# Row sums of |w_fc| taken by VectorE instead of ScalarE in a two-layer gated transformer kernel

## What is computed

```python
def _bitlinear(x, w_latent):
    scale = clip(mean(abs(w_latent), axis=1, keepdims=True), 1e-05, None)
    tern = clip(round(w_latent / scale), -1.0, 1.0)
    w = w_latent + stop_gradient(tern - w_latent)
    return x @ (w * scale).T

h = _bitlinear(x, w_fc) + gate * (x @ v.T @ fast_b.T @ u.T)
r = maximum(h, 0.0)
return _bitlinear(r * r, w_proj)
```

## Time and profile before

| | us |
|---|---|
| median of three runs | 1175.09 |
| lowest and highest | 1174.94, 1177.23 |
| span of the profiled execution, first to last instruction | 1176.7 |
| PE busy in it | 1094.3 (93%) |
| DVE busy | 953.5 (81%) |
| ACT busy | 799.4 (68%) |

### The profile page before, as it was taken

One profiled execution on the slowest core, in us unless ns is written; L12 is line 12 of the kernel. 1 busy time (PEld: TensorE's weight loads), 2 busy tenths in 40 slices (PEclk: granted clock), 3 DMA queues, 4 the chain that ended last, 5 costly groups with the idle time before them and its releaser, 6 DMA issues.

```text
span 1176.7 us, 22172 instructions
## 1 busy us (share of the span) xinstructions
PE 1094.3 (93%) x8270; PEld 677.4 (58%) x8558; DVE 953.5 (81%) x1989; ACT 799.4 (68%) x1575; POOL 591.5 (50%) x567
## 2 busy tenths in 40 slices
PE   5776699999999999999899999999999999999997
PEld 5544456474655656475655656475656656564654
DVE  4796868778789888788878798898879886998667
ACT  3988947676683958576584857676674957586545
POOL 4243545464653746454544656555545555564431
PEclk9888799999999999999999999999999999999999
DMA  9959651434525343533625252443436242432210
GB/s 339 367 153 309 204 122 47 99 81 77 126 59 117 69 116 73 104 81 68 126 53 136 57 123 68 89 110 77 108 55 145 45 119 61 103 69 55 68 45 27
DMA packets 273802, 128.11 MB, mean 109 GB/s; under 512 B 247568, under 2 KB 248080, under 8 KB 272016
## 3 DMA queue, kind: packets, MB, share of 16 engines
q1 hardware_dynamic: 273136, 125.73, 41.8%
q10 hardware_dynamic: 560, 0.96, 0.3%
HBM read 57.19 MB, written 8.39 MB: 56 GB/s over the span
## 4 chain that ended last, share of the span: by engine, by line
PE 55%; ACT 17%; DVE 16%; POOL 5%; issue 4%; DMA 2%; SPq 0%; ACTq 0%; DVEq 0%
PE ps L1861 14%; PE ps L1835 10%; PE ps L1904 6%; PE ps L1920 5%; PE ps L1788 5%; ACT e L966 4%; PE ps L1735 4%; PE ps L1883 4%; ACT rl L1002 3%; ACT hid L1007 2%; ACT sq L1013 2%; PE ps L1760 1%; DVE st L1369 1%; PE ps L1841 1%; PE ps L1775 1%
## 5 line engine op out<-in xcount | busy, mean ns | idle before, releaser
L1835 PE MATMUL ps<-xT,fcT 128*128 128x256 f16 x2048 | 262.5, 276 | 10.8 <-ACT rl L1002 7.1
L749 POOL TENSOR_TENSOR rs<-ve,nhalf 128x1 f32<-128x1 f32 x160 | 101.7, 638 | 306.1 <-DVE ve L1374 222.8
L1861 PE MATMUL ps<-pjT,hid 128*128 128x512 fp8e4 x1024 | 232.3, 379 | 2.6 <-POOL hid L776 1.6
L1835 PEld LDWEIGHTS ps<-xT,fcT 128*128 128x128 fp8e4 x2048 | 200.1, 99 | 52.6 <-ACT rl L1002 10.0
L776 POOL TENSOR_TENSOR hid<-sq,hid 128x512 f16<-128x512 f32 x128 | 163.1, 1279 | 80.3 <-ACT sq L1013 79.4
L1861 PEld LDWEIGHTS ps<-pjT,hid 128*128 128x128 f16 x1024 | 98.0, 98 | 98.3
L1002 ACT ACTIVATE rl<-ps,rsf 128x256 f32<-128x256 f32 x256 | 106.4, 469 | 25.0 <-PE ps L1841 24.8
L966 ACT ACTIVATE e<-ps,nmb,sig 128x128 f32<-128x128 f32 x256 | 113.1, 462 | 7.2 <-DVE nmb L1412 6.9
L1904 PE MATMUL ps<-w1T,q4T 128*128 128x512 fp8e4 x480 | 114.2, 379 | 0.7 <-issue 0.6
L1058 ACT ACTIVATE q<-h 128x2048 f16<-128x2048 f32 x30 | 57.3, 1910 | 79.3 <-DVE h L1531 79.3
L781 POOL TENSOR_TENSOR e<-e,einv 128x512 f32<-128x512 f32 x64 | 70.1, 1100 | 78.5 <-DVE einv L1416 78.5
(11 more groups left out here) (243 smaller groups left out, 2025.7 us busy)
## 6 DMA issues: line engine op xcount, KB each, us to landing
xb<-in_x SPq DMA_DIRECT2D x16, 512.0 KB, 3.6
xa<-in_x SPq DMA_DIRECT2D x15, 512.0 KB, 4.0
out<-r SPq DMA_DIRECT2D x30, 256.0 KB, 2.3
rope<-in_rope SPq DMA_DIRECT2D x16, 384.0 KB, 3.2
h<-in_w1T SPq DMA_DIRECT2D x6, 1024.0 KB, 5.8
h<-in_w2T SPq DMA_DIRECT2D x6, 1024.0 KB, 6.4
h<-in_wkvT SPq DMA_DIRECT2D x2, 1024.0 KB, 12.6
hid<-in_w_fc SPq DMA_DIRECT2D x2, 1024.0 KB, 9.9
```

The costliest lines, as they stand in the source:

```text
L1835: pe.matmul(ps[:, FFN0 + m % 2, a * G:(a + 1) * G], fcT[:, k, f * P:(f + 1) * P], xT2[:, xs, k, :], start=(xs == 0 and k == 0), stop=False)
L1861: mm = pe.matmul(ps[:, FFN0 + t, :], hid[:, xs, c, t * P:(t + 1) * P], pjT[:, c, :], start=(c == 0 and xs == 0), stop=(c == FC - 1 and xs ...
```

## The change

`row_sums` and its four places on ACT are gone, with the semaphore `c_rows`. `row_scales` on DVE now makes the sums of a "fc" piece itself, with one reduction over a view of 4 x 512 elements per partition, in front of scale and reciprocal, as it did for "pj". It waits for the piece's transfer instead of for ACT. The place numbers of all other steps are as they were, and no transfer is moved. The order of PE, POOL and SP is the same, instruction by instruction.

```diff
@@ PREP, ACT @@
-                     evac=(6, 14, 15, 29, 33, 35, 36, 37), rows=(4, 7, 10, 21), whole=(5, 8, 12, 28), low=(32,),
+                     evac=(6, 14, 15, 29, 33, 35, 36, 37), whole=(5, 8, 12, 28), low=(32,),
@@ ACT @@
-            def row_sums(q):
-
-                i = QUANT[q][1]
-                arrived(act, q)
-                src = piece[PLACE[q]]
-                for c in range(KC):
-                    done = KC * i + c
-                    if done > 0:
-                        act.wait_ge(c_rows, done)
-                    act.activation(lowA[:, c * D:(c + 1) * D], src[:, c * D:(c + 1) * D], ACT.Abs,
-                                   accum_out=scf[:, done:done + 1]).then_inc(c_rows, 1)
...
-                for q in here("ACT", "rows", p):
-                    row_sums(q)
                 for _ in here("ACT", "low", p):
-                    act.wait_ge(c_rows, FC)
@@ DVE, row_scales @@
                 kind, i = QUANT[q]
+                arrived(dve, q)
+                src = piece[PLACE[q]]
                 if kind == "fc":
                     sc, cols = scf[:, 4 * i:4 * i + 4], slice(4 * i, 4 * i + 4)
-                    dve.wait_ge(c_rows, KC * (i + 1))
+                    src = src.rearrange("p (c n) -> p c n", c=KC)
                 else:
                     sc, cols = scd[:, i:i + 1], slice(FC + i, FC + i + 1)
-                    arrived(dve, q)
-                    dve.tensor_reduce(sc, piece[PLACE[q]], axis=AX.X, op=ALU.add, apply_absolute_value=True).then_inc(c_rowd, 1)
-                    dve.wait_ge(c_rowd, i + 1)
+                dve.tensor_reduce(sc, src, axis=AX.X, op=ALU.add, apply_absolute_value=True).then_inc(c_rowd, 1)
+                dve.wait_ge(c_rowd, q + 1)
```

More of the change, by code:

```diff
@@ L258, in build @@
          c_krot, c_wmax, c_mxd, c_mxps, c_mx, c_wscale, c_whi, c_wlo, c_vrep, c_kvmax, c_kvinv, c_kap, c_khi, c_klo,
-         c_vhi, c_vlo, c_cs, c_csb, c_cps, c_cb, c_tanh, c_wchain, c_scale, c_b2, c_rows, c_thr, c_rowd, c_quant, c_quantg,
+         c_vhi, c_vlo, c_cs, c_csb, c_cps, c_cb, c_tanh, c_wchain, c_scale, c_b2, c_thr, c_rowd, c_quant, c_quantg,
          c_tern, c_quantp, c_lowps, c_low, c_lowzero, c_lowF, c_lowt, c_lowact, c_bnd, c_rsf, c_scd,
@@ L263, in build @@
             "c_wmax c_mxd c_mxps c_mx c_wscale c_whi c_wlo c_vrep c_kvmax c_kvinv c_kap c_khi c_klo "
-            "c_vhi c_vlo c_cs c_csb c_cps c_cb c_tanh c_wchain c_scale c_b2 c_rows c_thr c_rowd c_quant c_quantg c_tern c_quantp "
+            "c_vhi c_vlo c_cs c_csb c_cps c_cb c_tanh c_wchain c_scale c_b2 c_thr c_rowd c_quant c_quantg c_tern c_quantp "
             "c_lowps c_low c_lowzero c_lowF c_lowt c_lowact c_bnd c_rsf c_scd c_scps c_sc c_asum "
```

## The result

| | before | after |
|---|---|---|
| median of five runs, us | 1177.23 | 1184.04 |
| lowest and highest, us | 1174.94, 1179.34 | 1182.16, 1185.53 |
| span of the profiled execution, us | 1176.7 | 1181.9 |

The changed kernel is slower by a ratio of 1.0057, 95% interval 1.0040 to 1.0074: +6.7 us, between 4.7 and 8.7. The prediction said 1180.0 with a range of 1176.9 to 1181.6. The direction was right and the mechanism mostly too. The size was too small, and the range did not hold the time. The five runs of before include the three of the table ahead of the prediction, whose median was 1175.09, 2.1 us lower.

A forecast was written before the change was run, and what follows sets the result against it. PE, busy 93% of the span, was read as the bound, the change acting in the first 92 us. Terms +2.7, first collision +0.4, second +1.8 made +4.9 on 1175.1: 1180.0 us, range 1176.9 to 1181.6.

The forecast's parts named there:

- the 0.4 kept for it: VectorE's four-result reduction was taken as 2.3 us a piece; 0.4 us more per piece was kept for the range.
- here lies the trap: Piece 2: sums stand behind the maximum of v, which waits for PE; 1.4 us late at the scores of group 0.
- piece 3: No VectorE gap: 2.3 us in full, 3.7 us late; PE's mix covers 1.0, leaving 2.7 at the first w_proj sum.
- The first collision: First subtraction of P on VectorE starts 0.16 us before GpSimd's normalisation, which takes 0.4 us more.
- second collision: Third subtraction of P on VectorE held by GpSimd's w_proj conversion; VectorE stands still 2 us, +1.8 in the sum; chance 0.47.
- The race: At 77.4, GpSimd's conversion starts ahead of VectorE's third subtraction of P by 0.1 us or less.
- The "faster" rival: ScalarE's relief reaches the path at pieces 1 and 2, -0.7 us each; 1172 to 1173.7 us; chance 0.08.
- PE starts its transposes ... 0.5 us late: Piece 0: k's second rotation is pushed back about 0.5 us, so the first ternary block starts 0.5 us late.
- PE is now 0.5 late, so 37.9: Piece 2: the maximum of v, started when PE finishes v, moves from 37.38 to 37.9.
- the clock only behind 92 us: At 92.5 to 94 us PE's granted clock is 0.54; other waits could move that slow stretch a microsecond either way.
- The extra hold at the products behind v: Rival: GpSimd's second x16a subtraction holds two VectorE tensor_scalars behind the maximum of v; +0.95 us, 1180.9; no separate chance.
- If the delay at 91 us is not found at the end: Sign of being wrong: the delay at the last block of transposes, about 91 us, should reach the run's end one to one.

The follow-up runs named there:

- f4: Against e3, its eight extra PE matmuls included: GpSimd's second x16a subtraction moved behind its first sum of q's rotation; 1183.0 us, ratio 1.0058 to the kernel before.
- f1: Kernel before with piece 3's sums alone on VectorE, at the place of the change; 1179.27 us, +0.31%.
- e2: Changed kernel with piece 2's sums on VectorE moved ahead of the maximum of v; 1182.63 us, ratio 1.0049 to the kernel before.
- e3: Changed kernel with eight unused matmuls on PE behind the projection of k, before the first ternary block; 1184.89 us, ratio 1.0071 to the kernel before.
- f2: Changed kernel with piece 0's sums on VectorE moved ahead of the low half of wq; 1183.35 us, ratio 1.0064 to the kernel before.
- h1: Kernel before with piece 1 alone on VectorE, ScalarE's piece 2 passes moved up, GpSimd's second x16a subtraction moved later; 1176.53 us, ratio 0.9996.
- e4: Changed kernel with the third subtraction of P moved behind the sums of the second w_proj piece; 1180.87 us, +0.37% on the kernel before.
- f3: Changed kernel with piece 3's sums moved up into VectorE's gap after the second rotation of q; 1179.12 us, +0.19% on the kernel before.
- g1: Kernel before with the sums of pieces 1 and 2 shared, two blocks each on ScalarE and VectorE; 1177.29 us, +0.10%, interval around zero.
- g2: Changed kernel with eight extra PE matmuls, GpSimd's second x16a subtraction later, piece 3's sums in the gap after q's second rotation; 1179.95 us, +0.33% on the kernel before.
- g3: Kernel before with piece 3's sums alone on VectorE, in the gap after the second rotation of q; 1179.26 us, +0.30%.
- g4: Kernel before with piece 0's sums alone on VectorE, at its place of the changed kernel; 1176.65 us, +0.05%, interval around zero.
- e1: Changed kernel with piece 3's sums back on ScalarE, pieces 0 to 2 on VectorE; 1179.90 us, +0.30% on the kernel before.

## Why the prediction came out too low

**Right, by its own steps.** The reductions cost 2.25 to 2.29 us in the form with four results, without the 0.4 kept for it. Piece 2 "here lies the trap" held: VectorE's wait for v stood ahead of the sums, ScalarE idled 5.20 us before the conversion of piece 2, and where nothing else interferes (f4) the scores start at 54.97, forecast 54.9. At piece 3 the 2.3 us came in full and the mix covered 0.94. The first collision cost 0.36 (0.4). The second happened, with 2.0 us at the second w_proj sum; the prediction says that VectorE stands still for 2 us and then adds 1.8, without a reason for the difference. f1 showed the subtraction at the forecast length, 2.42 us. The race, to which the prediction gave a chance of 0.47, went the same way in all six traces with piece 3 at this place and the subtraction unmoved: the two sums start 5.18 us apart in after, e2, e3, f1, f2 and f4, to 0.01 us. The "faster" rival was rightly rare: with VectorE's wait for ScalarE's sums gone, VectorE waited for PE instead (h1).

The rule of the Trainium skill, page "SBUF — State Buffer", section "Who interferes with whom", agrees with all of these rows: the first to start keeps the pair, a lead of 0.08 us was enough (f1), and no tensor_reduce over a piece was stretched, also with GpSimd at work beside it (in after the one at 83.25 took 2.27 us beside GpSimd's conversion of 83.42 to 85.39).

**The step that failed first: the delay taken over by PE as it stood.** In "PE starts its transposes ... 0.5 us late" and "PE is now 0.5 late, so 37.9", I carried a delay of PE as a mere shift. In the profiled execution it also was a longer wait (2.62 us against 1.45), and after it the granted clock was 0.78 and 0.88: +1.6 us up to the maximum of v. The prediction spoke of the clock only behind 92 us, and of its paying. The same error came again at piece 3, where ScalarE's cast was 5.70 us late instead of 3.7, and at the end of the preparation: behind the second collision the clock was 0.72 from 80 to 92 us, and the delay grew by 0.9 us from the second sum to the last block. The clock also gave back: 0.75 us at the scores, 1.7 at the output projection (5.34 instead of 7.03 us). In the profiled pair this nets out: +6.85 at the last block, +5.2 at the end. That this is near the forecast +4.9 is luck, since neither the losses nor the returns were in the sum.

**The second step that failed: the hold was left out of the sum.** The extra hold at the products behind v stood among the rivals, at 0.95 us and without a chance of its own. With the clock at full speed it occurs in e3, e4, f2, f3 and g1, and the products take 0.48 to 0.61 us in all kernels where GpSimd's second subtraction comes later (f4, g2 and h1 by its place, f1, g3 and g4 because ScalarE's cast ahead of it stands behind the sums of piece 2). So piece 2 costs 0.8 us and besides either about 0.9 of hold or about 1.6 of clock, never the 0.9 alone that the sum had. That, and not the collisions, is the term that was mis-sized: +1.4 at the scores should have been +2.4 to +3.1 (counted from PE's first work, in after, e1, e3, e4, f2 and f3; 3.0 in after). From the scores to the last block the forecast was +3.5, and after has 3.75.

**The third: the base that the sum was put on.** The forecast is the median of three runs, 1175.09, plus 4.9. The median of five runs of the same kernel is 1177.23, and with more runs beside the experiments it came out at 1175.9 to 1177.1. Of the 4.0 us between 1180.0 and 1184.04, 2.1 are this base and 1.9 the size of the change. Either alone was enough to leave the range, though narrowly: 1175.1 + 6.7 = 1181.8, and 1177.2 + 4.9 = 1182.1, against 1181.6.

The relation of span and time was also misjudged. The five runs of after have both numbers, 1184.04 with a span of 1181.9, 1182.18 with 1180.1, and so on: the time is 2.1 us over the span, where the text ahead of the prediction has the median 1.6 us under it. A span of 1176.7 belongs to a time near 1178.8, so the profiled execution of before was one of its longer ones. From it the forecast would have been 1176.7 + 4.9 + 2.1 = 1183.7, and the profiled execution of after took 1184.04.

**Carry to the end.** "If the delay at 91 us is not found at the end" happened in part in the profiled pair, where 6.85 became 5.2. Over all fourteen changed kernels it did not. The sum of the three columns of the table is the last block's start after PE's first work. Its delay against before is 6.7 us in after and the time is 6.7 us longer; for e1 the two are 2.4 and 3.5, for f1 4.3 and 3.6, for f4 5.2 and 6.8, for h1 -1.0 and -0.5 (the times as the ratio less 1, on 1176 us). They agree within 2.2 us in every kernel, and on average the time is 0.5 us longer than the delay. So the delay does arrive, one to one as far as these runs can tell, and the shortfall of the sum lies before the last block. A single execution tells less: from the first down projection to the end the traces take 1025.5 (f3) to 1028.9 us (e3), although nothing was changed there, and g2's 3.9 us of time against 1.7 of delay stays unexplained.

## What to carry to other kernels

Before work is moved to an engine with idle time, look at what stands ahead of each new place in its queue: VectorE had 1.38 us of idle at piece 2, but behind a wait for PE, and none at piece 3. A delay of PE is not only a shift: here 0.7 us of delay, with a wait grown from 1.45 to 2.62 us, cost another 1.6 us in clock, and a delay of half a microsecond can start or stop a collision of VectorE with GpSimd, so each later pair of starts has to be worked out anew. And where the relieved engine (ScalarE, 17.7 of 19 us busy) paces nothing that PE is not pacing too, its relief buys little: 0.56 us at the scores in h1, and nothing in its time. A median of three runs is also a thin base for a forecast of half a per cent: here it moved by 2.1 us with two runs more.

## What the runs showed of the hardware

- A 4 x 512 reduction of 128 partitions costs what a flat one of 2048 does: 2.25 to 2.29 us against 2.25 to 2.28; half of it, 2 x 512, 1.21 us.
- With the same instructions, PE's projection of k took from 8.18 (after) to 9.81 us (g1) in the profiled executions of these kernels, and the first load, of `small`, let PE start at 8.28 to 10.23 us.
- The length of PE's last wait does not alone decide the clock. In front of the first ternary block 2.51 and 2.62 us were followed by the lower level and 2.08 was not. In front of piece 3's transposes 2.06 us were followed by it in after (16 transposes in 3.73 us), and 2.29 us in e4 and 2.72 us in e3 were not (there the first 8 took 1.09 and the next 8 1.23 or 1.24 us). What else counts was not tried.
- A hold by GpSimd seems to hit very small VectorE instructions too: with GpSimd at work beside it, the scale of four sums took 0.82 us in e2 and 0.42 in f2 instead of 0.17. No experiment moved GpSimd away from it.
